# A graph transformer of two layers on one core: experts written as loops, forward sums moved behind the first group, a slice attention with turned sums and three tiles in flight

## What is computed

```python
def _L0_gnn_ref(x, edge_index, ...):     # 80000 edges, both directions
    h_fwd = _sage(x, src, dst, W_l_f, b_l_f, W_r_f)
    h_bwd = _sage(x, dst, src, W_l_b, b_l_b, W_r_b)
    ...
def _L0_ffn_ref(x, Wr, W1s, b1s, W2s, b2s, W1p, b1p, W2p, b2p):   # F = 1024, 8 experts, 2 chosen
    shared = gelu(x @ W1s + b1s) @ W2s + b2s
    rw = softmax(x @ Wr)
    topw, topi = top_k(rw, 2)
    topw = topw / sum(topw)
    ...
    priv = einsum('bsef,efd->bsed', gelu(einsum('bsd,edf->bsef', x, W1p) + b1p), W2p) + b2p
    return shared + einsum('bsed,bse->bsd', priv, mask)
def _L1_ffn_ref(x, W_fx, ...):           # 8 heads of 64, 64 slices
    slice_weights = softmax((x_mid @ W_slice + b_slice) / temp)
    slice_norm = slice_weights.sum(axis=2)
    slice_token = einsum('bhnc,bhng->bhgc', fx_mid, slice_weights) / (slice_norm[..., None] + 1e-05)
    q, k, v = slice_token @ W_q, slice_token @ W_k, slice_token @ W_v
    attn = softmax(einsum('bhgc,bhkc->bhgk', q, k) * SCALE)
    out_x = einsum('bhgc,bhng->bhnc', einsum('bhgk,bhkc->bhgc', attn, v), slice_weights)
    return out_x @ W_out + b_out
```

## Time and profile before

| what | value |
| --- | --- |
| median of 3 runs (lowest, highest) | 2137.51 us (2136.07, 2140.94) |
| the profiled execution, its time | 2132.05 us |
| its span in the profile | 2130.3 us |
| PE, DVE, ACT, POOL busy over the span | 84%, 51%, 39%, 12% |
| granted clock of TensorE, mean | 0.929 |
| graph windows, 50 to 497: DVE, PE busy | 415.39, 388.47 of 447 us |
| scatter, 40 transfers of POOL (L1684) | 1024.56 to 1075.5 |
| gathers, 40 transfers of POOL (L1689) | 1467.78 to 1517.7 |
| MAX8, FIND_INDEX8 on DVE | 1.46, 2.7 us for 20 each |
| shared blocks 0 to 2 end; block 3 begins; 4 ends | 1145.2; 1465.6; 1560.6 |
| last TensorE row of ln3 | near 1910.8 |
| slice: 21 loads issued by SP | 1912.34 to 1923.48 |
| slice tiles, first logits to last sums (L2191) | 1935.6 to 2051.1 |
| a tile on PE: L2179, L2187, L2190, L2191 | 1.7, 0.5, 1.7, 0.9 us |
| a tile on DVE: 5 operations of 128x512, a reciprocal | 0.69 each, 0.20 |
| a tile on ACT: exponent (L2239), copy (L2241) | 0.63, 0.60 us |
| table loads of ACT in the slice tiles | 10 of 1.28 us, every second tile |
| slice_out ready; last projection | 2086.0; 2090.2 to 2127 |

### The profile page before, as it was taken

The page is one execution under the profiler, slowest core; times in us unless marked ns, Lnnn a source line. Parts: engine busy times, 40 slices in busy tenths (PEclk is TensorE's granted clock), DMA queues, the critical chain, the costliest instruction groups (busy, mean ns, idle before and its releaser), DMA issues. The chain is left out here.

```text
span 2130.3 us, 34130 instructions
## 1 busy us (share of the span) xinstructions
PE 1784.7 (84%) x9535; PEld 1098.3 (52%) x9536; DVE 1084.6 (51%) x3108; ACT 831.9 (39%) x1831; POOL 260.3 (12%) x340
## 2 busy tenths in 40 slices
PE   6888888887858999998669999999559857976867
PEld 4234444445636423335437999997244446433436
DVE  7999988886488663334201000000347652334662
ACT  3456777773113475663112444433113233001312
POOL 2000000000092000000510000003300022201102
PEclk9999999999978999998879999999679978987988
DMA  2001111116440000002241112121110001411001
GB/s 73 0 26 60 51 75 75 75 75 212 132 138 1 1 1 1 1 1 81 77 138 40 59 60 96 59 96 56 55 40 0 0 8 67 137 64 31 0 0 51
DMA packets 87011, 117.78 MB, mean 55 GB/s; under 512 B 7404, under 2 KB 73263, under 8 KB 86927
## 3 DMA queue, kind: packets, MB, share of 16 engines
q1 hardware_dynamic: 81614, 105.62, 14.6%
q0 software_dynamic: 3936, 10.37, 1.5%
q10 hardware_dynamic: 1376, 0.66, 0.1%
HBM read 69.75 MB, written 46.87 MB: 55 GB/s over the span
## 5 line engine op out<-in xcount | busy, mean ns | idle before, releaser
L691 PE MATMUL bank<-onehot_key,onehot_low 128*128 128x320 bf16 x1720 | 320.3, 302 | 58.6 <-DVE onehot_key L505 23.4
L505 DVE TENSOR_SCALAR onehot_key<-iota_keys,edge_keys 128x640 bf16<-128x640 f16 x860 | 313.2, 385 | 0.0
L691 PEld LDWEIGHTS bank<-onehot_key,onehot_low 128*128 128x128 bf16 x1720 | 123.2, 97 | 241.6 <-DVE onehot_key L505 216.5
L504 DVE TENSOR_SCALAR onehot_low<-iota_low,edge_low,window_offset 128x128 bf16<-128x128 f16 x645 | 205.8, 319 | 33.0 <-PE bank L691 26.2
L1827 ACT ACTIVATE hidden<-bank,b_cols 128x128 f32<-128x128 f32 x344 | 126.5, 368 | 178.5 <-PE bank L1761 155.2
L1761 PE MATMUL bank<-slot_columns,w 128*128 x1376 | 163.6, 278 | 3.3 <-issue 3.3
L1914 DVE COPY slot_columns<-bank 128x256 f32 x43 | 18.3, 425 | 290.6 <-PE bank L1767 290.6
L1761 PEld LDWEIGHTS bank<-slot_columns,w 128*128 128x128 f32 x1376 | 163.2, 195 | 5.7 <-issue 3.5
L1767 PE MATMUL bank<-w,hidden 128*128 128x256 f32 x688 | 155.6, 379 | 0.0
L1767 PEld LDWEIGHTS bank<-w,hidden 128*128 128x128 f32 x688 | 127.4, 190 | 15.5
L570 ACT ACTIVATE low_distance<-iota_window,edge_low_negated 128x128 f32<-128x128 f32 x215 | 86.6, 403 | 112.0 <-PE bank L691 110.7
(11 more groups left out here) (475 smaller groups left out, 2870.3 us busy)
## 6 DMA issues: line engine op xcount, KB each, us to landing
AT_dram<-at_strip SPq DMA_DIRECT2D x20, 640.0 KB, 4.0
A_dram<-a_strips SPq DMA_DIRECT2D x20, 640.0 KB, 3.0
sg_strip<-AT_dram SPq DMA_DIRECT2D x20, 640.0 KB, 3.9
back_strip<-A_dram SPq DMA_DIRECT2D x24, 480.0 KB, 7.0
w<-in_L_ffn_W1p SPq DMA_DIRECT2D x8, 1024.0 KB, 4.9
w<-in_L_ffn_W2p SPq DMA_DIRECT2D x8, 1024.0 KB, 7.6
slot_rows<-ty_zero SPq DMA_DIRECT2D x1, 6144.0 KB, 23.7
slot_columns<-slot_rows SPq DMA_DIRECT2D x12, 512.0 KB, 8.9
```

Of the source, the lines that this page charges most:

```text
L504: dve.tensor_scalar(ohl[:, q, :], iow[:, :], lowc[:, ds(c, 1)], woff[:, ds(w, 1)], ALU.subtract, ALU.is_equal)
L505: dve.tensor_scalar(ohk[:, q, :], ioh[:, :], key[:, ds(c, 1)], None, ALU.is_equal).then_inc(s_key[q], 1)
L691: last = pe.matmul(bank[2 * (x % 2) + h][:, 0:HB], ohl[:, q, :], ohk[:, q, h * HB:(h + 1) * HB], start=start and q == 0, stop=q == Q - 1, ...
```

## The change

- **graph and backward.** The forward sums of `x` 1 to 4 stand behind a window's first group, not behind its loop. The bias additions leave the windows; GpSimd adds them per cut in `backward_stage` for one direction, VectorE in one operation at the start of `forward_h` for the other.
- **ln1, experts.** The router's logits come block by block in two banks, and VectorE sorts them within ln1. TensorE waits for the counts and makes the ranks before the shared blocks. These are hardware loops over blocks on TensorE, ScalarE and VectorE, with six hidden banks for all. The mask, its turning and the 9-row products are gone; `b2` is loaded broadcast over 128 partitions (9 tensors of 128 KB), added once to all of `X` by VectorE and, for each expert, in place of the copy of a routed tile. `combine` is a loop over tiles.
- **projections.** Written out, no staging, columns read in place, six banks.
- **slice.** Loads are issued in ln3 (15 instead of 21). Tiles are written out, with three banks of logits and three buffers. The slice weights are the stationary side of the sums, and rows with a column of ones behind them (257) move. No staged columns. The tail divides by counts per partition, turns the sums, makes q, k, v in one wide product each, and divides the attention at the end; ScalarE shares its copies.

```diff
@@ graph_stage, TensorE's window
                             group(before, True)
                             following = load_next()
+                            t = i * 2 + k
+                            if t >= 1 and x:
+                                forward(t - 1, 1 - k, x)
                             with pe.Fori(before + 1, following[0]) as n:
                                 group(n, False)
...
                                 turn(t - 1, 1 - k, x)
-                                forward(t - 1, 1 - k, x)
+                                if x == 0:
+                                    forward(t - 1, 1 - k, x)
@@ backward_stage
+                            dve.wait_ge(s_bias, j + 1)
...
                         def forward_h():
+                            dve.tensor_tensor(part(XN, 0), part(XN, 0), spread(bl[:, 0:P], 1, T), ALU.add)
@@ experts_stage, TensorE
+                        def shared(blocks, buf, arrived, routed_tiles=None):
+
+                            with pe.Fori(*blocks) as b:
...
+                                for f in range(FB):
+                                    if 2 <= f < 6:
+                                        pe.wait_ge(s_yf, b * WT + (f - 1))
+                                    if f >= 6:
+                                        pe.wait_ge(s_g, b * FB + (f - 5))
...
+                                pe.wait_ge(s_g, b * FB + FB)
+                                for j in range(WT):
+                                    for f in range(FB):
+                                        last = pe.matmul(bank[2 + j][:, 0:C], hid[:, f, j * P:(j + 1) * P], w2[buf][:, f, :],
+                                                         start=f == 0, stop=f == FB - 1)
+                                    last.then_inc(s_y, 1)
...
+                        pe.wait_ge(s_cnt, 3)
...
+                        shared((0, EARLY), 0, 32)
@@ experts_stage, VectorE
+                        st.then(dve.tensor_tensor(X[:, :, :], X[:, :, :], spread(b2[:, 0, :], 1, T), ALU.add))
...
+                                dve.tensor_tensor(XS[:, t, :], bank[4][:, 0:C], b2[:, ds(e + 1, 1), :].rearrange("p o c -> p (o c)"), ALU.add).then_inc(s_rc, 1)
@@ project_stage, TensorE
+                        for t in range(T):
+                            if t >= NBANK:
+                                pe.wait_ge(s_add, t - NBANK + 1)
@@ slice_stage, TensorE
+                        def logits(t):
+                            if t >= DEEP:
+                                pe.wait_ge(s_sub, t - DEEP + 1)
...
+                            for p in range(IB):
+                                last = pe.matmul(bank[4 + p][:, 0:C + 1], pr[k][:, p * P:(p + 1) * P], xs[t % 2][:, :], start=t == 0, stop=t == T - 1)
+                            last.then_inc(s_zt, 1)
...
+                        for t in range(DEEP):
+                            logits(t)
+                        for t in range(T):
+                            sums(t)
+                            if t + DEEP < T:
+                                logits(t + DEEP)
```

More of the change, by code:

```diff
@@ L787, in _ @@
                         sp.wait_ge(s_next, 16 * len(loads))
+                    @block.gpsimd
+                    def _(pool):
+                        for lo, hi in cuts:
+                            pool.tensor_tensor(part(XN, 1, slice(lo, hi)), part(XN, 1, slice(lo, hi)), spread(bl[:, P:2 * P], 1, hi - lo), ALU.add).then_inc(s_bias, 1)
                     @block.tensor
@@ L1064, in _ @@
                     def _(pool):
[L1065 to L1082 removed]
+                        pool.wait_ge(s_w, 16)
@@ L1695, in _ @@
                         pe.transpose(bank[7][:, 0:NX * FB], b1r[:, :], ident[0:NX * FB, 0:NX * FB]).then_inc(s_b, 1)
-                        def hidden_bank(b, f):
-                            return bank[f % 6] if b == 0 else bank[f % 2]
-                        def turn_weights(b):
-                            for j in range(WT):
-                                last = pe.transpose(bank[6 + b % 2][0:NX, j * P:(j + 1) * P], mk[:, b * WT + j, :], ident[:, :])
-                            last.then_inc(s_mt, 1)
@@ L1934, in _ @@
+                        for g in range(T // GG - 1):
+                            combine(g)
+                        shared((NB - 1, NB))
                         combine(T // GG - 1)
@@ L2180, in logits, with sums @@
                             last.then_inc(s_lg, 1)
-                        def sums(t, k, first, final):
+                        def sums(t):
+                            k = t % DEEP
+                            pe.wait_ge(s_p, t + 1)
+                            if t:
+                                pe.wait_ge(s_pc, t)
+                            for p in range(IB):
+                                last = pe.transpose(bank[3][:, p * P:(p + 1) * P], pr[k][:, p * P:(p + 1) * P], ident[:, :])
+                            last.then_inc(s_pt, 1)
@@ L2191, in sums @@
-                            last = pe.matmul(bank[7][:, :], ones[1 if final else 0][:, :], pr[k][:, :], start=first, stop=final)
-                            last.then_inc(s_zt, 1)
-                        pe.sem_inc(s_pc, 1)
-                        pe.sem_inc(s_zt, 2)
-                        pe.sem_inc(s_lg, 2)
-                        logits(0, 0)
-                        logits(1, 1)
-                        sums(0, 0, True, False)
-                        with pe.Fori(0, T // 2 - 1) as i:
-                            for k in range(2):
-                                logits(i * 2 + (k + 2), k)
-                                sums(i * 2 + (k + 1), 1 - k, False, False)
```

628 lines of the change are left out of this document (291 added, 337 removed).

## The result

| | before | changed |
| --- | --- | --- |
| median of the runs taken together | 2136.79 us | 2042.09 us |
| lowest to highest (4 runs each) | 2134.34 to 2140.94 | 2041.39 to 2045.77 |
| span of the profiled execution | 2130.3 us | 2044.0 us |

The account below looks back on a forecast made before the run. No one engine bounds the kernel, so each edit is worth what its stage lets through. Gains 15+27+14+10+8+16 = 90 us take 2132 to 2042, shifted by 5.5 to 2047 us; range 1985 to 2067.

Parts of the forecast that it names:

- Slice, before the tiles: Slice stage up to the first logits: weights loaded in ln3 end the waits for them; gain 15 us.
- tiles: Slice tiles: with three in flight TensorE bounds at 4.1 us a tile, where a pair took 10.90; gain 27 us.
- R2: Rival at the slice tiles: a buffer keeps the pair at 10.90 us, so they gain nothing; 2074 us, chance 0.09.
- Tail with the last projection: Slice stage's end: wide matmuls and dropped head-by-head operations gain 14 us, the last projection's earlier start 4.
- Projects: Projections: no ScalarE staging and no TensorE wait for bias; last one 4 us, la_out 6, together 10.
- Graph: Graph windows: moved forward sums save a third of VectorE's 26 us of slot waits; gain 8 us, ends 0 and 20.
- Experts: Experts stage: ranks first, no bias matmuls, b2 added by VectorE, loops; gain 16 us, ends 6 and 69.
- (i): Experts, ranks first: TensorE starts its shared block at about 1012.8 instead of 1008.43; slots ready some 7 us sooner.
- (iii): Experts: VectorE adds b2, 6 us beside TensorE; in routed tiles a 0.42 us addition replaces a 0.425 us copy.
- (ii): Experts: bias matmuls go, a give takes 3.72 us instead of 4.27; 20 mask transposes go (2.7 us).
- (a): Experts stalls: indirect transfers delay reports of TensorE's finished instructions, limiting its run-ahead; stalls stay, 2047 us, chance 0.50.
- (b): Experts stalls: TensorE's code fetches stand behind indirect transfers; loops end both stalls, experts gain 69 us, 1995 us, chance 0.33.

Follow-up runs that it names:

- combined: Changed kernel with shared-block loops written out, b2 addition cut by block, rank matmuls behind block 0's third hidden group; 1980.11 us, ratio 0.9581.
- half_indirect: Changed kernel with only the first of each tile's two indirect scatters and two gathers (20 and 20 instead of 40 and 40); 1981.63 us.
- half_scatter_plain_gather: Changed kernel with 20 of the 40 scatters left out and the gathers replaced by plain transfers that SyncE issues; 1977.09 us.
- forward_only: Kernel before with one edit: forward sums of windows 1 to 4 behind the first edge group; 2056.32 us against 2067.25, ratio 0.995.
- the control: Changed kernel once more, unedited, beside the kernel before on a later chip; 1984.86 us against 2066.21, ratio 0.9607.

## Why the prediction was right, and where not

**The time** came out 4.9 us from the forecast. Part of that nearness is luck: the experts gave 7 us where I wrote 16, the graph 14 where I wrote 8, the tail 12 where I wrote 18, and Taylor attention's 4.9 us are no effect of the change. That the stalls would come again with nearly the same length was a guess too, since their cause was not known; they did in the runs predicted for, and in no later one.

**Slice, before the tiles** (15, measured 14.0) and **tiles** (27, measured 25.8): right. The period of 4.1 us was a sum of TensorE's rows and became 3.95, one table load is left of ten, and the fill was 12.3 us instead of 10.2. "A slice tile takes over 5 us" did not happen; R2 is gone.

**Tail with the last projection** (14 + 4, measured 12.0): mis-sized. I took three wide matmuls at 2.6 us and no clock. The rows of the changed kernel:

```profile
1987.63 0.88 DVE L2277 COPY sl_tok<-bank 64x256 f32<-64x256 f32 x2 [7.59 <-PE bank L2165]
1988.57 4.28 PE L2169 MATMUL bank<-sl_tok,w_slice_qkv 128*128 128x512 f32 x6 [0.97 <-DVE sl_tok L2277]
```

and the windows of this stretch in the changed kernel and in `combined`:

```profile
1980.00:1993.00 13.00, 11.70 (x32) 7.28 (x33) 1.70 (x5) 1.19 (x2) 0.00 (x0) 0.61 0.00 0
```

```profile
1923.00:1932.00 9.00, 7.70 (x34) 4.83 (x35) 1.88 (x5) 1.19 (x2) 0.00 (x0) 1.00 0.00 0
```

The clock granted was 0.61, a mean of the two levels, and the same matmuls that take 4.28 us there take 2.84 at 1.00. The tail from the last turned tile is 28.0 us in one case and 23.7 in the other, so 4.3 of my missing 6 us are the clock. It fell in the short dependent steps of the tail, but in three of the eleven profiled runs with this tail (`combined`, `half_indirect`, `half_scatter_plain_gather`) it stayed up through the same steps; what decides it is not shown.

**Projects**: la_out 7.0 for 6, right. **Graph** (8, measured 14.1): mis-sized twice. "I take a third of 26" for the order: it took 14 of the 26 us of waits away and gave 10 to 11 us. And "the bias additions leave GpSimd's 0.7 us per tile, hidden anyway" was the step that failed: hidden from the waits, they lengthened VectorE's own operations, 8 us in all. The vector addition in `forward_h` was indeed covered, within 1.6 us.

**Experts** (16, measured 7.2). In the first runs, from the router's end to the turns, 137.7 us became 126.4, 11.4 gained of the 13 in my sum. From the last routed hidden matmul to the kv matmuls, 132.0 became 133.1, 1.2 lost where I wrote 3 gained (and my own terms there, 2 + 2.5 - 3, make 1.5). The router's stage lost 3.2 at a lower clock, as it also did in `forward_only`. Even the 11.4 are two errors that cancel: the stall ended 72.6 us after the router's end against 73.7 before, not 7 us sooner, but more was done in it, so that 53.7 us were left to the turns and not 57 to 58. Where no stall blurs it (`forward_only` against the control), from the router's end to the kv matmuls, it is +5.6 (ahead of block 0), -12.3 (blocks 0 to 2), -5.7 (blocks 3 and 4), +7.1 (behind them): 5.3 us gained; in the first runs the stalls were 3.9 us shorter on top. (i) TensorE starts 5.6 us later against the router's end, near my 4.4. "The slots are ready some 7 us sooner" was right by itself (11.2 us after the router's end instead of 17.5), but the second transfer is only 1.3 us sooner (0.4 in the first runs), because the first one takes 6.21 us. A step that failed is (iii), "VectorE adds b2 instead: 6 us beside TensorE": I checked it against TensorE and not against GpSimd, which was issuing. (ii) The shorter gives: -12.3 and -5.7, where 0.55 for each of 12 and 8 gives, the mask transposes (2.7) and the rank matmuls that moved ahead (0.9) make 10.2 and 4.4; TensorE's busy time there falls by 13.2 and 5.8, so it is all matmul work and no shorter wait. And "a loop with a wait per operation, costs 3 more" was 7.1: 1.98 us a tile in place of 1.16, and not only for the last five, since 15 tiles now last 30.5 us and make VectorE 2.5 us late for block 4.

**Readings (a) and (b)**: (a)'s forecast held in the runs that were predicted, but (a) as a mechanism is not shown. Neither had a place for what the runs show: that the stalls may not be there at all. I argued about code and transfers from a single trace.

## What to carry to other kernels

Where a stall is bound to one place in a trace, run the same kernel again, on another chip, before explaining it by the code: some 70 of this kernel's 2137 us were there in the first runs and on none of the three chips tried later. And see whether the trace of the stall is whole: a releaser that the program does not wait for, or a transfer without a landing, can mean that events are missing. When work moves between VectorE and GpSimd, look at the durations of the other's operations beside it, not only at waits: each held the other here, in both directions. Put a burst of matmuls where the consumers have a buffer in hand, not behind a loop, and keep short dependent VectorE operations grouped by kind and not looped by tile, when they end a stage.

## What the runs showed of the hardware

- The kernel before takes 2137 us in the first runs and 2061 to 2067 on three chips later. In the first runs TensorE, some 150 instructions after indirect transfers began, stood (34.57 us) or got one matmul and its weight load through per 1.4 to 2.8 us, until 4 to 6 us after the last transfer; later never. The two traces of the first runs lack landing events of each of these transfers.
- An indirect transfer of GpSimd that meets a VectorE operation of 5.49 us takes 6.21 us instead of 1.25, and 2.08 beside one of 1.23 us. A plain transfer of GpSimd beside the same 5.48 us takes 0.81.
- The reverse: a GpSimd addition of 0.7 to 0.8 us lengthens the VectorE one-hot beside it by 0.41 to 0.50 us, with no wait in the profile.
- The same router matmuls (80) and the norm around them took 15.9 us at a granted clock of 0.71 and 18.7 at 0.59, in either kernel, from run to run:

```profile
992.00:1008.00 16.00, 15.99 (x107) 15.89 (x104) 3.69 (x11) 3.86 (x7) 0.00 (x0) 0.71 0.59 208
```

```profile
978.00:997.00 19.00, 18.98 (x107) 18.89 (x105) 3.54 (x10) 3.85 (x7) 0.00 (x0) 0.59 0.49 172
```

The first is the kernel before in the profile shown, the second `forward_only`, whose code is the same there. A stage of 20 us can differ by 3 us with no cause in the program. Three stages did so here (router 3.2, Taylor attention 4.9, slice tail 4.3 us), and each looked like an effect of the change.
